# Two fused attention layers, 32 images: softmax reciprocals written to memory in 16-byte pieces and read back with a stride, input load and split moved by one to two slots

## The reference

```python
# layer 0, per image; g = x as (128, 1024), d = 64
t = W_theta @ g + b_theta ; p = W_phi @ g + b_phi          # (64, 1024)
f = softmax(t.T @ p / sqrt(64), axis=-1)                   # (1024, 1024)
x = x + W_fuse @ (g @ f.T) + b_fuse
# layer 1, per image
h = group_norm(x, 32 groups) * gn_w + gn_b
q, k, v = q_w @ h + q_b, k_w @ h + k_b, v_w @ h + v_b      # (128, 1024)
a = softmax(q.T @ k / sqrt(128), axis=-1)
x = x + p_w @ (v @ a.T) + p_b
```

## Time and profile before

| what | value |
|---|---|
| time before, median of 3 runs | 2479.89 us (2476.52 to 2480.52) |
| the profiled execution: its time | 2480.26 us |
| its span, first to last instruction | 2478.5 us |
| mean granted TensorE clock over the span | 0.904 of full speed |
| PE, DVE, ACT, POOL busy | 1926.6, 1587.0, 1570.7, 1538.9 us |
| SP waiting at L318 for the write of the reciprocals | 866.8 us, 124 waits |
| median from issue to landing of that write | 10.1 us |

### The profile page before, as it was taken

How to read it: one execution, slowest core, us unless ns; L and a number is a source line. 1 busy time by engine, 2 the same in 40 slices (tenths; PEclk the granted TensorE clock), 3 DMA queues, 4 the chain that set the end, 5 groups by cost and what they waited for, 6 DMA issues and landing times.

```text
span 2478.5 us, 33388 instructions
## 1 busy us (share of the span) xinstructions
PE 1926.6 (78%) x8388; PEld 1525.2 (62%) x8388; DVE 1587.0 (64%) x1706; ACT 1570.7 (63%) x2281; POOL 1538.9 (62%) x1605
## 2 busy tenths in 40 slices
PE   5778778787878777787777787877787777877876
PEld 4656666566666666666666565666666666666654
DVE  4656666666676666666666665766666666756653
ACT  4656667666666666566666666666666666766643
POOL 3566656667566666557665666665666665665654
PEclk8888899899899899898998998998988899988988
DMA  5699999999999999999999999999999999999994
GB/s 89 88 123 124 108 116 130 117 112 121 124 116 114 128 118 105 124 120 116 111 123 121 116 117 128 115 114 125 120 108 122 126 107 125 128 110 111 122 99 81
DMA packets 909238, 286.32 MB, mean 116 GB/s; under 512 B 871457, under 2 KB 872353, under 8 KB 909217
## 3 DMA queue, kind: packets, MB, share of 16 engines
q1 hardware_dynamic: 909216, 286.08, 97.5%
HBM read 50.86 MB, written 17.04 MB: 27 GB/s over the span
## 4 chain that ended last, share of the span: by engine, by line
DMA 50%; SPq 36%; issue 8%; PE 3%; ACT 1%; POOL 1%; DVE 1%; POOLq 0%; DVEq 0%; ACTq 0%
DMA rden_dram<-rden 47%; SPq L296 28%; DMA pair_t<-pair 2%; SPq L351 2%; SPq L321 2%; SPq L341 1%; PE s_ps L372 1%; SPq L331 1%; PE o_ps L372 1%; DMA xs<-in_x 1%; PE s_ps L408 0%; PE m_ps L372 0%; POOL et L755 0%; ACT et L576 0%; ACT s_ps L565 0%
## 5 line engine op out<-in xcount | busy, mean ns | idle before, releaser
L755 POOL TENSOR_SCALAR et<-pair_t 128x2048 fp32r<-128x2048 f16 x384 | 733.3, 1910 | 756.4 <-DMA pair_t<-pair 752.9
L372 PE MATMUL o_ps<-et,v_hi 128*128 128x512 f32 x2048 | 821.7, 444 | 183.2 <-POOL v_lo L771 154.5
L631 DVE TENSOR_REDUCE neg_max<-s_ps 128x1 f32<-128x1024 f32 x512 | 623.1, 1217 | 430.8 <-PE s_ps L372 419.2
L372 PEld LDWEIGHTS o_ps<-et,v_hi 128*128 128x128 f32 x2048 | 425.8, 208 | 279.1 <-POOL v_lo L771 145.9
L648 DVE SCALAR_TENSOR_TENSOR pair<-s_ps,pair 128x1024 f16<-128x1024 f32 x384 | 467.7, 1218 | 48.0 <-ACT pair L588 46.8
L588 ACT ACTIVATE pair<-s_ps 128x1024 f16<-128x1024 f32 x384 | 392.9, 1023 | 102.1 <-DMA pair_t<-pair 84.1
L372 PE MATMUL o_ps<-et,v_lo 128*128 128x512 f32 x1024 | 437.5, 427 | 0.0
L565 ACT ACTIVATE s_ps<-s_ps,neg_max 128x1024 f32<-128x1024 f32 x384 | 416.7, 1085 | 19.9 <-DVE neg_max L631 13.8
L372 PE MATMUL s_ps<-phi,theta 128*128 128x512 f32 x1024 | 324.8, 446 | 8.1 <-DMA phi<-phi 4.8
L642 DVE SCALAR_TENSOR_TENSOR et<-s_ps,et 128x1024 fp32r<-128x1024 f32 x128 | 156.8, 1225 | 223.3 <-ACT et L576 220.4
L372 PEld LDWEIGHTS s_ps<-phi,theta 128*128 128x128 f32 x1024 | 228.0, 224 | 65.1 <-issue 5.3
(11 more groups left out here) (89 smaller groups left out, 2477.3 us busy)
## 6 DMA issues: line engine op xcount, KB each, us to landing
rden_row<-rden_dram SPq DMA_DIRECT2D x128, 256.0 KB, 5.0
xs<-in_x SPq DMA_DIRECT2D x32, 512.0 KB, 4.3
phi<-phi SPq DMA_DIRECT2D x64, 256.0 KB, 4.6
out_y<-y_sb SPq DMA_DIRECT2D x64, 256.0 KB, 2.5
pair_t<-pair SPq DMA_TRANSPOSE x384, 4.7
rden_dram<-rden SPq DMA_DIRECT2D x128, 2.0 KB, 10.1
w_f<-in_w_fuse_t SPq DMA_DIRECT2D x1, 64.0 KB, 2.7
ident_sb<-in_ident SPq DMA_DIRECT2D x1, 64.0 KB, 2.2
```

The lines of the kernel that those rows point to most:

```text
L372: mm = pe.matmul(out, lhs_t, rhs, start=start and n == 0, stop=stop and n == len(terms) - 1)
L631: nc.vector.tensor_reduce(neg_max[:, t % 4:t % 4 + 1], s_ps[:, part(t), :], AX.X, ALU.max, negate=True).then_inc(s_max, 1)
L755: return nc.gpsimd.tensor_scalar(*args)
```

## The change

The layout of `rden_dram` is turned round. Before, one group was stored as 4 rows of 128 numbers (tile, query), so a partition's 4 reciprocals went to 4 places, as 512 pieces of 4 bytes. Now it is stored as (query, tile), and a partition's 4 numbers lie side by side: 128 pieces of 16 bytes. The bytes read back are the same 2 KB, in one run, but in the order (query, tile), so the product on DVE now reads `rden_row` in steps of 4 numbers (16 bytes) with an access pattern of three dimensions. Apart from this the copy of `xs` to `xr` moves from slot 3 to slot 1, the load of `xs` from 4 to 2, the making of `x_hi` from 7 to 6 and of `x_lo` from 8 and 10 to 7 and 9.

```diff
-X_SLOT = 7
-X_LO_SLOTS = (8, 10)
-XR_SLOT = 3
-XS_SLOT = 4
+X_SLOT = 6
+X_LO_SLOTS = (7, 9)
+XR_SLOT = 1
+XS_SLOT = 2
...
-        rden_dram = nc.dram_tensor("rden_dram", (2, GROUP, P), F32).ap()
+        rden_dram = nc.dram_tensor("rden_dram", (2, P, GROUP), F32).ap()
...
-                sp.dma_start(rden_dram[g].rearrange("t q -> q t"), rden[:, g, :],
-                             allow_slow_non_contiguous=True).then_inc(s_rden_dram[g], 16)
+                sp.dma_start(rden_dram[g], rden[:, g, :]).then_inc(s_rden_dram[g], 16)
...
-                             rden_dram[g].rearrange("t q -> (t q)").partition_broadcast(P)).then_inc(s_rden_row[g], 16)
+                             rden_dram[g].rearrange("q t -> (q t)").partition_broadcast(P)).then_inc(s_rden_row[g], 16)
...
-                nc.vector.tensor_tensor(to[:, cols], o_ps[:, :], rden_row[:, g, :], ALU.mult).then_inc(s_taken, 1)
+                nc.vector.tensor_tensor(to[:, cols].rearrange("c (t q) -> c t q", t=GROUP),
+                                        o_ps[:, :].rearrange("c (t q) -> c t q", t=GROUP),
+                                        rden_row[:, g, :].rearrange("c (q t) -> c t q", t=GROUP), ALU.mult).then_inc(s_taken, 1)
```

## The result

The changed kernel takes 2158.89 us (median of 4 runs, 2154.83 to 2160.34), the kernel before 2478.77 beside it. The ratio is 0.871 with an interval of 0.869 to 0.872: 320 us less. The forecast was 2080, with a range of 1990 to 2230.

The account below looks back on a forecast made before the run. SP's wait for the reciprocals' write was taken as the bound; with it gone, DVE's account (2480.3 - 419.2 = 2061) and PE's (2153, less 74 of clock, 2079) meet at about 2080 us; range 1990 to 2230.

Parts of the forecast that it names:

- The bound: SP's queue, waiting 866.8 us for the write of the reciprocals to land, sets the pace; any landing under 7.0 us suffices.
- The write: Reciprocals to memory, 512 pieces of 4 bytes become 128 of 16: landing falls from 10.1 to 4.0 us.
- lower bound: Shortest landing expected of the new write: 2.5 us, as for a 256 KB store and the load of `vec`.
- let the rest go by the number of pieces: Landing of the write: a fixed 2.0 us, the remainder divided by 4 with the pieces, giving 4.0 us.
- rival 1: The write goes by memory touched, not pieces: landing 8.5 to 10.1 us, time 2275 to 2480 us; 7%.
- Rival 2: Landing between 7.0 and 8.5 us, or POOL still late behind transposes: 2230 to 2290 us; 4%.
- The standstill: While the write is in flight, DMA engines are occupied but move 17 GB/s; the transpose issued behind it stands too.
- DVE's account: DVE's work and waits once PE's scores are never late: 2480.3 less 419.2 gives 2061 us.
- PE's account: PE without its waits for POOL (289.2) and half of h_lo's (37.6): 2153 us; 74 of clock back gives 2079.
- The product: DVE's multiplication by the reciprocals, now in 16-byte steps: taken at 0.68 us; doubled, 1.36, at most 87 us in all.
- The moves: Earlier load and split of x: secure the 106.2 us of x_lo already in PE's account; price taken as 0.
- What is late next: With SP on time, its waits for `pair` and for POOL's output sum (13.2 us before) were expected to grow.

Follow-up runs that it names:

- the pairs: Changed kernel with a group's tiles stored in two pairs (256 pieces of 8 bytes, product read in steps of 8 bytes): 2051.0 us, ratio 0.881 to kernel before.

## Why the prediction was right, and where it was off

**The bound.** SP's queue was the bound and the write's landing its cause: right. Giving SP its wait back without touching the write brought 193 us. Of the change, the layout alone brought 165 on its chip (2329.2 to 2163.7), the product's loss included, and the slots alone lost 24.

**The write.** I took 4.0 us from the number of pieces and 2.5 as the lower bound; it is 1.4. What failed here is "let the rest go by the number of pieces", and the reading by places touched, rival 1, failed too: the same 512 pieces land in 9.1 or 2.1 us, depending on how closely they lie. It did no harm, because any landing under 7.0 us was enough, and that sentence held; that the landing came out far under it was luck as far as the reasoning goes. Why the rows of the lower bound stand at 2.5 us was not looked into; one is a store of 256 KB, the other a load. Rival 2 was also laid out wrongly: by the prediction's own 128 us for each 1 us, a landing of 7.0 to 8.5 is 2083 to 2275 us and not 2230 to 2290.

**The standstill** of the transpose behind the write was read rightly from the earlier trace rows. With SP's wait away at most 84 us are its cost, which the prediction didn't part from SP's wait.

**DVE's account (2061).** It let all 419.2 us of waiting for scores go. 195.5 stayed, because PE now waits for DVE (163.9 us, it was 29.9), and the two take turns. Yet DVE's idle time fell by 410 us, nearly as in the sum, and this was luck: the waits for theta and k_lo, which the account had left standing, fell by 118, and the one for ACT's part of the turned tile, which was to stay, by 45. What lifts DVE's account to the measured time is its work, 84 us more (1587.0 to 1671.4): 49 in the products and 40 in the residual. **PE's account (2153, and 2079 with clock).** Its three waits on POOL went as said (v_lo 0.2, x_lo 10.4, et 2.1), but the one for DVE's low half took up part of their place, so that PE's idle time fell by 223 us and not by 327. The clock gave back more than I had assumed: from 19% of the span at the lower level to 9%, and PE's busy time fell by 103 us where I had taken 74. That the span is 2153 us, the account's value without the clock, is chance.

**The product.** I took 0.68 and kept 1.36 as the other end; it is 1.07. This is the term that was mis-sized: 110 us with what follows from it, against 0 in the sum and 87 in the range. Without it the kernel takes 2051, and the forecast of 2080 lies between that and 2159. The lines of 16 bytes of the Trainium skill, "SBUF — State Buffer", section "Door 1: The DMA port swizzle", were right in direction, and the measured steps agree (8 bytes 691 ns, 16 bytes 1049). The same section of the Trainium skill says that one can stride for free by 4 numbers of fp32; taken as a step of 16 bytes this does not hold here. What I missed is that a longer DVE instruction moves the next one into POOL's way; no estimate of the product alone would have found the 42 us.

**The moves.** I counted them as securing the 106.2 us of x_lo. They secure nothing: the wait vanishes with the old slots too (11.1 us), since POOL is no longer late. The price that I put at 0 is 0 with the new layout and 24 us with the old; whether the load, `xr` or the split costs these was not tried.

**What is late next.** I named SP's wait for `pair` and for the output sum. The first grew to 421.8 us and the second to 24.8 only; the largest of the rest, the wait for the reciprocals of DVE (313.5), I had not named.

## What to carry to other kernels

Here the queue that issues transfers hardly ever waited for an engine, and it was the bound. Before the transfer is made faster it is worth asking whether its wait can simply stand later: here one number did more than the change as made (193 us and 166), though less than the pairs (278). Small pieces of 4 bytes written side by side by many partitions were slow because they lay close, so give each more bytes or its own place. And when a layout is changed for one end, look at the other: splitting the difference (8-byte pieces, step of 8 bytes) kept both ends fast, and was worth 5% over the change as made.

## What the hardware showed that I had not expected

- 128 writes of 4 bytes side by side land in 8.2 us, spread to 512 bytes each in 1.4 us; 512 of them in 9.1 and 2.1 us.
- This landing differed between the result and chip B: 10.1 and 9.2 us, and with it the kernel before by 6% (2479 and 2328 us), of which the landing explains about three quarters. The changed kernel was the same on both (2159 and 2162).
- DVE reads fp32 in SBUF in steps of 8 bytes for free (691 ns for 512 elements, as contiguous), in steps of 16 for 1049, and writes in steps of 16 for 1058. A step of 16 bytes in PSUM is free.
- A residual of 0.75 us took 2.43 because it started 0.01 us after POOL's conversion; starting 0.37 us before it, it took 0.95, and the conversion 2.34 instead of 1.90.
